# Cross attention in a six-layer decoder: one head of each key group in a step, scores as 32-row tiles four side by side, keys split once in a trip

## What is computed

```python
H, KV, HD = (16, 4, 96)
G = H // KV
hidden = jnp.concatenate([context, latents], axis=1)       # 256 rows: 128 of context, 128 of x
q = (latents @ Wq.T).reshape(b, q_len, H, HD)
k = (hidden @ Wk.T).reshape(b, s_len, KV, HD)
v = (hidden @ Wv.T).reshape(b, s_len, KV, HD)
q = q.transpose(0, 2, 1, 3).reshape(b, KV, G, q_len, HD)
scores = jnp.einsum('bkgqd,bksd->bkgqs', q, k) * scale
attn = jax.nn.softmax(scores, axis=-1)
out = jnp.einsum('bkgqs,bksd->bkgqd', attn, v)
out = out.reshape(b, H, q_len, HD).transpose(0, 2, 1, 3).reshape(b, q_len, H * HD)
return out @ Wo.T
```

## Time and profile before

| | us |
|---|---|
| median of 3 runs | 851.04 |
| lowest, highest | 850.72, 855.27 |
| the profiled execution | 849.07 |
| its span in the profile | 847.3 |
| granted clock of PE, mean | 0.998 |
| PE busy | 812.5 (96%) |
| DVE busy | 574.4 (68%) |
| ACT busy | 432.6 (51%) |
| POOL busy | 262.2 (31%) |

### The profile page before, as it was taken

One profiled execution on the slowest core, in us unless ns is written; L12 is line 12 of the kernel. 1 busy time (PEld: TensorE's weight loads), 2 busy tenths in 40 slices (PEclk: granted clock), 3 DMA queues, 4 the chain that ended last, 5 costly groups with the idle time before them and its releaser, 6 DMA issues.

```text
span 847.3 us, 22622 instructions
## 1 busy us (share of the span) xinstructions
PE 812.5 (96%) x9288; PEld 673.8 (80%) x9288; DVE 574.4 (68%) x1510; ACT 432.6 (51%) x1109; POOL 262.2 (31%) x310
## 2 busy tenths in 40 slices
PE   6999999999999999999998999999999999999996
PEld 6888887675557787777776789988989899989993
DVE  5675666586876666677776547983767566756776
ACT  4454444568763343465555446634644475347532
POOL 0221522579976532112222567710000100010001
PEclk9999999999999999999999999999999999999999
DMA  8410002222221200010000122320000010000001
GB/s 306 142 53 16 16 22 83 66 70 56 72 63 38 63 22 9 20 29 18 19 19 19 32 62 89 100 65 26 1 2 2 1 50 2 2 1 27 2 2 50
DMA packets 20998, 36.77 MB, mean 43 GB/s; under 512 B 3200, under 2 KB 7424, under 8 KB 20640
## 3 DMA queue, kind: packets, MB, share of 16 engines
q1 hardware_dynamic: 20800, 35.20, 13.6%
q10 hardware_dynamic: 96, 0.13, 0.1%
HBM read 30.86 MB, written 2.10 MB: 39 GB/s over the span
## 4 chain that ended last, share of the span: by engine, by line
PE 78%; DVE 10%; ACT 4%; issue 2%; POOL 2%; DMA 2%; SPq 1%; ACTq 0%; POOLq 0%; DVEq 0%
PE bank L833 18%; PE bank L835 16%; PE bank L834 16%; PE bank L984 6%; PE bank L1259 5%; PE bank L1004 2%; PE bank L1121 2%; DVE tank L2565 2%; PE bank L989 2%; DVE tank L2345 1%; PE bank L954 1%; PE bank L1108 1%; PE bank L1243 1%; DMA x_all<-x_dram 1%; PE bank L1278 1%
## 5 line engine op out<-in xcount | busy, mean ns | idle before, releaser
L833 PE MATMUL bank<-wr,hTl 128*128 128x512 f32 (+3 forms) x392 | 153.5, 391 | 1.3 <-issue 0.8
L835 PE MATMUL bank<-wr,hTh 128*128 128x512 f32 (+3 forms) x392 | 147.0, 375 | 0.0
L834 PE MATMUL bank<-wr,hTh 128*128 128x512 f32 (+3 forms) x392 | 146.6, 374 | 0.0
L1562 ACT ACTIVATE pT<-bank 128x512 f32<-128x512 f32 x128 | 70.0, 605 | 94.9 <-PE bank L954 94.9
L2345 DVE TENSOR_REDUCE tank<-bank 128x4 f32<-128x512 f32 x128 | 82.0, 682 | 42.4 <-PE bank L954 42.4
L833 PEld LDWEIGHTS bank<-wr,hTl 128*128 128x128 f32 (+1 forms) x392 | 73.7, 188 | 17.7 <-issue 5.3
L835 PEld LDWEIGHTS bank<-wr,hTh 128*128 128x128 f32 (+1 forms) x392 | 73.7, 188 | 12.6
L834 PEld LDWEIGHTS bank<-wr,hTh 128*128 128x128 f32 (+1 forms) x392 | 73.8, 188 | 11.3 <-issue 1.0
L833 PE MATMUL bank<-hTh,wr 128*128 128x256 f32 (+1 forms) x272 | 82.0, 302 | 0.0
L834 PE MATMUL bank<-hTl,wr 128*128 128x256 f32 (+1 forms) x272 | 81.3, 299 | 0.0
L835 PE MATMUL bank<-hTh,wr 128*128 128x256 f32 (+1 forms) x272 | 81.2, 298 | 0.0
(11 more groups left out here) (257 smaller groups left out, 1923.8 us busy)
## 6 DMA issues: line engine op xcount, KB each, us to landing
raw<-w_qkv_dram SPq DMA_DIRECT2D x12, 256.0 KB, 2.8
raw<-w_xq_dram SPq DMA_DIRECT2D x16, 192.0 KB, 2.3
raw<-w_xo_dram SPq DMA_DIRECT2D x12, 256.0 KB, 2.8
cin<-xT_dram SPq DMA_DIRECT2D x8, 256.0 KB, 3.6
x_all<-x_dram SPq DMA_DIRECT2D x8, 256.0 KB, 7.0
cin<-ctx_dram SPq DMA_DIRECT2D x8, 256.0 KB, 3.4
cin<-ctxT_dram SPq DMA_DIRECT2D x8, 256.0 KB, 2.9
out_dram<-x_all SPq DMA_DIRECT2D x8, 256.0 KB, 2.0
```

What stands on the lines that cost most here:

```text
L833: mm(dst, lhs[1], rhs[0], start=start, stop=False)
L834: mm(dst, lhs[0], rhs[1], start=False, stop=False)
L835: return mm(dst, lhs[0], rhs[0], start=False, stop=stop)
L1562: av(pT[e][:, 2 * rows + n, :], t_bank[n][:, :], ACT.Exp).then_inc(exp_ready, 1)
```

## The change

A step now takes one query head of each of the four key groups, for both slots. The features of a head are cut into three parts of 32, and the parts of the four heads lie in the four quarters of the 128 partitions. So the scores of four heads are four matmuls with 32 rows each, on four different quarters, into four different banks. Queries and keys come out of PE in that order (the weights are permuted outside), so they are copied and split in whole tiles, and the keys are split once in a trip.

```diff
-            def cross_scores(trip, s, g):
-                pe.wait_ge(xks_ready[s], nth(trip, XKV, g + 1))
...
-                if g > 0:
-                    pe.wait_ge(xo_ready[s], nth(trip, XKV, g))
-                for i in range(2):
-                    for j in range(2):
-                        ins = mm3(bank[s][i][:, j * XT:(j + 1) * XT], (hi[:, 2 * i + j, s, :], lo[:, 2 * i + j, s, :]), xks[s], True, True)
-                    ins.then_inc(xs_psum[s], 1)
+            def cross_scores(trip, g):
+                pe.wait_ge(xk_ready, nth(trip, PARTS_OF_HEAD, PARTS_OF_HEAD))
+                pe.wait_ge(xq_ready, nth(trip, XG, g + 1))
+                for q_lo, k_lo in ((1, 0), (0, 1), (0, 0)):
+                    q = xq_of(trip, g)[q_lo]
+                    for c in range(PARTS_OF_HEAD):
+                        for s in both:
+                            for n in range(XKV):
+                                at = rows_of_group(n)
+                                ins = mm(scores_bank(n)[:, s * XT:(s + 1) * XT], q[at, c, s, :], xk_parts[c][at, k_lo, s, :],
+                                         start=q_lo == 1 and c == 0 and s == 0, stop=q_lo + k_lo == 0 and c + 1 == PARTS_OF_HEAD,
+                                         skip_group_check=True)
+                ins.then_inc(xs_psum, 1)
...
+            def cross_probsT(trip, s, g):
+
+                pe.wait_ge(xp_ready[1], nth(trip, 2 * XG, 2 * g + 1 + s))
...
             def cross_values(trip, s, g):
...
+                if g + 1 < XG:
+                    pe.wait_ge(xq_ready, nth(trip, XG, g + 2))
+                if g + 2 == XG and trip > 0:
+                    pe.wait_ge(xT_hi[s], turned(trip - 1, FF))
...
+            def cross_keys(trip):
+
+                for n_done, i in enumerate(KEY_TILES):
+                    dve.wait_ge(xk_hi, nth(trip, PARTS_OF_HEAD, n_done + 1))
+                    v.tensor_tensor(xk_parts[i][:, 1, :, :], bank[i % 2][i // 2][:, :].rearrange("p (s t) -> p s t", s=SLOTS),
+                                    f32(xk_parts[i][:, 0, :, :]), ALU.subtract).then_inc(xk_ready, 1)
+
+            def cross_max(trip, g):
+                dve.wait_ge(xs_psum, nth(trip, XG, g + 1))
+                for n in range(XKV):
+                    r = stats[:, :, ROWMAX.start + n]
+                    steps_done(XA, trip, v.tensor_reduce(r, scores_bank(n)[:, :].rearrange("p (s t) -> p s t", s=SLOTS), AX, ALU.max))
+                    v.tensor_scalar(stats[:, :, NEGMAX.start + n], r, -(XD ** -0.5), None, ALU.mult).then_inc(xmax_ready, 1)
...
+                for n, s in ((0, 0), (0, 1), (1, 0), (1, 1), (2, 0), (3, 0), (2, 1), (3, 1)):
+                    act.wait_ge(xmax_ready, nth(trip, XKV * XG, XKV * g + n + 1))
```

More of the change, by code:

```diff
@@ L1214, in cross_q @@
                             pe.wait_ge(w_split, FREE + PIECES_XQ[g - 1] + KT)
+                        if g > 1:
+                            for s in both:
+                                pe.wait_ge(xo_ready[s], nth(trip, XG, g - 1))
                     for k in range(KT):
@@ L1244, in cross_probsT @@
                     ins.then_inc(xpT_psum[s], 1)
-            def quarters(tile):
-                return [(row + part, j, first + part) for at, row, j, first, n in places if at == tile for part in range(0, n, NARROW)]
             def cross_values(trip, s, g):
-                pe.wait_ge(xpT_ready[s], nth(trip, 2 * XKV, 2 * g + 2))
+                pe.wait_ge(xpT_ready[s], nth(trip, 2 * XG, 2 * g + 2))
                 if g == 0:
                     pe.wait_ge(xv_ready[s], nth(trip, 2, 2))
-                for tile in range(XG * XD // P):
+                if g + 1 < XG:
+                    pe.wait_ge(xq_ready, nth(trip, XG, g + 2))
+                if g + 2 == XG and trip > 0:
+                    pe.wait_ge(xT_hi[s], turned(trip - 1, FF))
+                for c in range(PARTS_OF_HEAD):
                     for t in range(2):
[L1257 to L1260, removed]
+                        for n in range(XKV):
+                            at = t * NKV + n * XD + c * PART
+                            ins = mm(values_bank(s, g)[rows_of_group(n), c * P:(c + 1) * P], xv[s][:, at:at + PART],
+                                     xpT[s][:, (2 * n + t) * P:(2 * n + t + 1) * P], start=t == 0, stop=t == 1)
                 ins.then_inc(xo_psum[s], 1)
@@ L1274, in routes_and_low @@
                 pe.wait_ge(xT_hi[s], turned(trip, FF))
+                if trip + 1 < TRIPS:
+                    pe.wait_ge(xo_ready[s], nth(trip + 1, XG, XG - 1))
                 if trip == 0:
@@ L1421, in _ @@
                 for g in range(XKV):
-                    each(cross_scores, trip, g)
+                    cross_scores(trip, g)
                     if g + 1 < XKV:
@@ L1722, in cross_keys @@
                 for n_done, i in enumerate(KEY_TILES):
[L1723 to L1731, removed]
+                    act.wait_ge(xk_psum, nth(trip, PARTS_OF_HEAD, n_done + 1))
+                    copy(xk_parts[i][:, 0, :, :], bank[i % 2][i // 2][:, :].rearrange("p (s t) -> p s t", s=SLOTS)).then_inc(xk_hi, 1)
             def cross_kept_values(trip, s, n):
@@ L1753, in cross_q @@
[L1753 to L1773, removed]
+                copy(hi[:, 2, :, :], third_part(trip, g)).then_inc(xq_hi, 1)
@@ L1791, in cross_heads @@
                 n = XG * XD // P
[L1792 removed]
+                copy(hTh[:, 0:n, s, 0, :], tiles(values_bank(s, g)[:, 0:XG * XD], n)).then_inc(xo_hi[s], 1)
             def route_exp(trip, s):
@@ L1906, in _ @@
                 for g in range(XKV):
-                    each(cross_probs, trip, g)
-                    if g == 0:
-                        cross_split(trip, 0, 1)
+                    cross_probs(trip, g)
                     if g + 1 < XKV:
@@ L1919, in _ @@
                     for s in both:
-                        if g + 1 < XKV and (g, s) != (0, 0):
-                            cross_split(trip, s, g + 1)
                         if g + 2 == XKV and behind and s == 0:
@@ L2743, in _ @@
                     cross_q(trip, 0)
-                each(cross_split, trip, 0)
+                cross_keys(trip)
                 for g in range(XKV):
-                    each(cross_max, trip, g)
+                    cross_max(trip, g)
                     if g + 1 == XKV and behind:
```

100 lines of the change are left out of this document (43 added, 57 removed).

## The result

The changed kernel takes 857.63 us (median of 7 runs, 856.48 to 861.49), the kernel before 851.59 (7 runs, 850.44 to 855.27): a ratio of 1.0069, 95% interval 1.0049 to 1.0089. It is slower, by 6.0 us; the forecast was 856.4.

What follows compares the result with a forecast made beforehand. PE was taken to bound the kernel, level with DVE in step 0. Trips 1 to 3 (+1.3) and trip 0 (+4.1) made +5.4 on the profiled 849.07, 854.5; 2.0 more gave a median of 856.4 us, range 850 to 869.

Steps and rivals of the forecast that it cites:

- The tiles: Cross attention scores on PE: 72 tiles at 28.5 ns, a block of 2.25 us, saving 0.66 us in steps 1 to 3.
- Three side by side: Rival, scores on PE: only three tiles run together, 39 ns each, +12 us, 868.5; chance 0.13 for three or fewer.
- The wait: Scores to DVE: one semaphore starts DVE's first maximum 2.35 us after the scores' start instead of 0.91, 1.44 later.
- Step 0 in trips 1 to 3: Start of scores to cross_values, set by DVE's chain: 10.79 us against 8.93, a loss of 1.86.
- Step 3: Trips 1 to 3, scores to cross_values with the routing on DVE: 10.77 us against 10.89, a gain of 0.1.
- Trips 1 to 3: Cross attention, all four steps summed: +0.44 us a trip, +1.3 us for the three trips.
- the gain of steps 1 and 2: Trips 1 to 3, where PE's own work follows the scores: 0.66 us gained in each, 1.32 together.
- the key splittings at no cost: In cross_keys, behind the keys' matmuls: covered by PE's values work, so free; without the cover 1.4 us a trip.
- Trip 0: Cross attention beside POOL's weight splitting: losses of 2.1, 0.3, 0.9 and 0.8 us, +4.1; between +0.5 and +4.1.
- DVE gets its time back in trip 0: Rival: the shift moves normings into POOL's pauses, giving back up to 3.6 us, down to 851.6; chance 0.15.
- The clock falls: Rival: PE's clock falls in the four steps 0, doubling the cross_values behind them, up to +11 us, 867; chance 0.06.
- The saving stays: Rival: DVE's chain in steps 0 and 3 has unseen slack, so PE's 10 us are net, 841; chance 0.08.

Runs made afterwards that it cites:

- the padding of step 0: Changed kernel with 6 more matmuls of 256 columns (0.7 us of PE) ahead of the next queries in step 0 of every trip: 856.71 us.
- the kernel where ACT copies more: Changed kernel; step 0 writes cross_values into a free bank, ACT copies both slots' probabilities there, and slot 0's in step 3 and all trip 0: 848.98 us.

## Why the prediction was right

**The tiles.** Forecast 28.5 ns a tile and a block of 2.25 us; measured 28.9 ns (16 in 0.46 to 0.47; 72 tiles make 2.1 us, and the way in and out 0.23) and 2.32 us. The pitch lies between the two bounds, 27.5 and 29.5. The block is 2.91 - 2.32 = 0.59 us shorter in steps 1 to 3, not 0.66. Three side by side, 39 ns, is out; so is the 38 ns that the prediction worked out from the 3.07x of the Trainium skill, "TensorE: Matmul & The Clock Gate", Part 3, for a run of 72 tiles as here.

**The wait.** First maximum at 2.35 forecast, 2.44 measured. Step 0 in trips 1 to 3: 10.79 forecast, 10.81 measured, by the chain as it was written; the loss is 10.81 - 8.93 = 1.88 us, forecast 1.86 (1.84 in the step's length, 13.57 - 11.73). PE stood for 1.46 us just before `cross_values`, where the prediction had it wait for some 2 us: the rest of its slack lies ahead of and between the transposes, which wait for the normings. Step 3: 10.77 forecast, 10.79 measured. That a late start and the place of the next queries each cost time is shown by a run of its own.

**Trips 1 to 3** were forecast at +0.44 each and came at +0.77, +0.70 and +0.49. The mis-sized term is the gain of steps 1 and 2: 1.32 forecast, while 15.39 and 16.47 against 15.92 and 17.01 make 1.07 in trip 1; it was 1.10 in trip 2 and 1.32 in trip 3, where step 1 of the kernel before was one of those that are 0.22 longer. A further 0.1 lies ahead of the scores, where the prediction had put the key splittings at no cost (602.91 - 574.16 against 595.92 - 567.27).

**Trip 0**: +4.1 forecast, +4.14 measured. That is luck: two errors cancel. Step 0 was forecast 12.1 from start to `cross_values` and took 13.3, since I took over the 7.4 us of maxima and normings; with the shift they fell on POOL's subtractions otherwise and took 526.34 - 517.76 = 8.6. Step 2 was forecast 15.2 and took 13.87, since its last normings fell behind POOL's end (maxima and normings 559.27 - 550.40 = 8.9 instead of 10.5), which I had named as the way down to +0.5. Steps 1 and 3 (13.1 and 9.87, forecast 13.3 and 9.8) were right.

**The rivals.** *DVE gets its time back in trip 0*: half right in step 2 and the reverse in step 0; where POOL's and DVE's instructions meet is no constant that a shift takes along. *The clock falls*: in the profiled execution it did, in trip 0 step 0 alone, and cost some 0.4 us of `cross_values` there, not in trips 1 to 3 (1.00 in 606 to 614 us, PE busy for 6.36 of 8). By the lower mean clocks the other runs may have lost more to it. *The saving stays* is refuted by the padding of step 0. *Three side by side* is refuted by the pitch. The sentence behind it, on the emptying of PSUM, fits in part: of DVE's 8.3 us from the first maximum to the last copy 2.9 are normings, from SBUF to SBUF, and most of the loss is the late start.

**The median** came 1.2 us above the forecast: the stretch gave 6.1 where 5.4 was forecast; the rest, 0.5, is the forecast's starting point (851.07 against 851.59). As an account of the median this sum is only as good as the profiled executions, whose clocks were 0.998 and 0.997.

## What to carry to other kernels

Before packing matmuls that feed another engine, look when that engine gets its first piece, not how long the block is: 24 matmuls in four portions let DVE start after 0.91 us, 72 faster ones with one signal after 2.44. The block's gain of 0.5 us became a loss of 1.9 in step 0, where DVE's chain sets the end: 1.5 by the later start, the rest by the order on DVE. Then move work off that chain (copies to an engine with slack, a bank that needs no wait) before counting the saving; here this turned +6 into some -3 us in the medians, -2 in the stretch. A term taken from a stretch where two engines disturb each other needs a range of its own, for a shift of 1.5 us changed it by 1.2 us upwards in one step and by 1.6 downwards in another.

## What the runs showed of the hardware

- A DVE instruction from SBUF to SBUF on two numbers a partition lasted up to 1.23 us instead of 0.17 beside POOL, and ended with POOL's instruction; instructions that read PSUM kept their time. A POOL fill of 384 columns took 0.42 us where the subtraction took 1.0, and DVE's maxima and normings in that step took 6.5 us with it instead of 8.6.
- Going from whole-array matmuls to 32-row tiles and back cost 0.11 and 0.12 us (the first 16 tiles took 0.58 us instead of 0.47; the last 8 of a block 0.35 instead of 0.23).
- In the kernel where ACT copies more, PE was busy for 2.16 of the 5 us from 520 us on and the granted clock was 0.50 in the 3 us behind them, 1.2 GHz throughout; in another execution 1.4 us of added matmuls ahead of that gap kept it at 1.00.
